# Two batches of near values and a tile's constant rows moved to GpSimd, across the border between two stages of a two-layer language-model kernel

## The reference, cut to what matters

```python
windows = [max(4, BLOCK_SIZE // 2 ** h) for h in range(H)]      # 256, 128, 64, 32, 16, 8, 4, 4, ...
qk = x @ Wqk + bqk
q, k = split(qk);  v = k                                        # the values are the keys
att = softmax(where(j <= i and j > i - window[h], q @ k.T / 4, -inf))
out = att @ v
gates = softmax(x @ Wgate + bgate)                              # one gate for each head
return (out * gates) @ Wproj + bproj
```

## Time and profile before

| | |
|---|---|
| median of the runs | 1427.9 us |
| profiled execution: its time, its span | 1427.86 us, 1426.1 us |
| PE, DVE, ACT, POOL busy | 1232.4, 849.3, 650.3, 666.0 us |
| mean granted TensorE clock | 0.925 of full |
| project_local, last PE instruction to last DVE instruction | 635.4 to 662.3 us |
| attend, first DMA to last DVE instruction | 662.8 to 801.9 us |

### The profile page before, as it was taken

The page is one execution under the profiler, slowest core; times in us unless marked ns, Lnnn a source line. Parts: engine busy times, 40 slices in busy tenths (PEclk is TensorE's granted clock), DMA queues, the critical chain, the costliest instruction groups (busy, mean ns, idle before and its releaser), DMA issues. The chain is left out here.

```text
span 1426.1 us, 29279 instructions
## 1 busy us (share of the span) xinstructions
PE 1232.4 (86%) x9695; PEld 967.0 (68%) x9696; DVE 849.3 (60%) x1794; ACT 650.3 (46%) x1253; POOL 666.0 (47%) x616
## 2 busy tenths in 40 slices
PE   6886999999978959972899796999689999989996
PEld 3664555555546747761667584999668888878885
DVE  5997788888827948996555494744323333333332
ACT  3881666666655635430354463333123333333332
POOL 7855777777361213787100000455225545444553
PEclk9995899999999977775999998999889999999998
DMA  2588999999400006563444320011275343545331
GB/s 56 172 255 264 253 273 276 278 282 270 111 2 1 1 28 184 173 202 94 91 113 95 110 83 30 23 30 37 68 268 133 55 110 80 139 129 137 51 53 19
DMA packets 122867, 179.27 MB, mean 126 GB/s; under 512 B 26052, under 2 KB 83820, under 8 KB 122772
## 3 DMA queue, kind: packets, MB, share of 16 engines
q1 hardware_dynamic: 105876, 159.62, 38.4%
q0 software_dynamic: 16896, 18.44, 7.9%
HBM read 104.73 MB, written 74.31 MB: 126 GB/s over the span
## 5 line engine op out<-in xcount | busy, mean ns | idle before, releaser
L1635 DVE TENSOR_REDUCE att_top<-att_psS 128x4 f32<-128x512 f32 (+2 forms) x192 | 195.2, 1037 | 46.8 <-PE att_psS L1522 43.7
L2791 POOL DMA_INDIRECT out<-ffn1c_y,ffn1c_table x72 | 113.3, 1574 | 180.8 <-ACT ffn1c_y L2904 92.1
L2932 DVE TENSOR_TENSOR ffn1c_hid<-ffn1c_psG,ffn1c_sil 128x512 f32<-128x512 f32 x72 | 49.8, 692 | 146.5 <-PE ffn1c_psG L2832 146.5
L1606 ACT ACTIVATE att_prob<-att_psS 128x1024 f32<-128x1024 f32 (+1 forms) x96 | 83.3, 888 | 64.9 <-PE att_psS L1536 64.9
L1516 PE MATMUL att_psS<-pairs_ka,pairs_qa 48*128 48x384 f32 (+3 forms) x512 | 100.3, 400 | 12.3 <-DMA pairs_ka<-k_parts 7.8
L2832 PE MATMUL ffn1c_psG<-ffn1c_w_h,ffn1c_xh 128*128 x288 | 97.9, 422 | 11.6 <-DMA ffn1c_w_l<-experts_lo 5.7
L1606 ACT ACTIVATE pairs_part<-att_psS 128x1024 f32<-128x1024 f32 (+1 forms) x96 | 82.8, 888 | 35.5 <-PE att_psS L1536 35.5
L2435 POOL DMA_INDIRECT slots<-ffn1b_entry,ffn1b_sloti x64 | 63.3, 989 | 65.7 <-ACT ffn1b_act_h L2648 54.1
L2780 POOL DMA_INDIRECT ffn1c_rows<-normed_rows,ffn1c_table x72 | 71.1, 987 | 45.4 <-DVE ffn1c_gate L2952 21.3
L2832 PE MATMUL ffn1c_psG<-ffn1c_w_l,ffn1c_xh 128*128 x288 | 91.5, 399 | 0.0
L2832 PE MATMUL ffn1c_psG<-ffn1c_w_h,ffn1c_xl 128*128 x288 | 91.3, 399 | 0.0
(11 more groups left out here) (397 smaller groups left out, 3505.4 us busy)
## 6 DMA issues: line engine op xcount, KB each, us to landing
prep_raw<-in_w_all SPq DMA_DIRECT2D x27, 512.0 KB, 5.4
experts_hi<-ffn0w_room SPq DMA_DIRECT2D x27, 512.0 KB, 5.6
experts_lo<-prep_lo SPq DMA_DIRECT2D x27, 512.0 KB, 6.6
ffn1c_w_h<-experts_hi SPq DMA_DIRECT2D x8, 1536.0 KB, 7.0
ffn1c_w_l<-experts_lo SPq DMA_DIRECT2D x8, 1536.0 KB, 11.4
qkv_near<-near_keys SPq DMA_DIRECT2D x32, 320.0 KB, 4.3
q_parts<-pairs_part SPq DMA_DIRECT2D x8, 1024.0 KB, 4.1
k_parts<-pairs_part SPq DMA_DIRECT2D x16, 512.0 KB, 5.9
```

Of the source, the lines that this page charges most:

```text
L1606: act.activation(dst, src, ACT.Exp, scale=0.25).then_inc(s["exp"], 1)
L1635: dve.tensor_reduce(dst, src, AX.X, ALU.max).then_inc(s["max"], 1)
L2791: pool.indirect_dma_start(out=rows_out, in_=y[:, t.buf, :], in_offset=None, out_offset=bass.IndirectOffsetOnAxis(ap=table[:, t.value:t.val ...
L2932: dve.tensor_tensor(hid[:, t.par, :], psG[:, t.par, 1, :], sil[:, t.par, :], ALU.mult).then_inc(s["act"], 1)
```

## The change

It has four parts.

1. `near`, `pv` and `pw` are allocated outside of both stages, so that they outlive `project_local`. POOL does the near values of batches 0 to 5 in `project_local`; those of batches 6 and 7 move to the start of POOL's list in `attend`. DVE's copy of the function, and its three instructions, are gone.
2. POOL's `third_term(7)` no longer waits for `near_products(7)`. For batches 0 to 6 that wait stays.
3. The four memsets of the constant rows go from DVE's list in `attend` to the front of POOL's.
4. PE waits for them at the first "B" of the block, and no longer ahead of its first "A".

Nothing of the shared expert is touched by the diff.

```diff
@@ project_local, POOL
             for b in range(B):
-                pool.wait_ge(s["prod"], b + 1)
+                if b < B - 1:
+                    pool.wait_ge(s["prod"], b + 1)
                 third_term(b)
-                if b >= 1:
+                if 1 <= b < B - 1:
                     near_values(b - 1)
-            pool.wait_ge(s["pv3"], B - 1)
+            pool.wait_ge(s["pv3"], B - 2)
+            pool.wait_ge(s["l"], B)
@@ project_local, DVE
-            def near_values(b):
-                dve.wait_ge(s["sdone"], 3 * b + 3)
-                dve.wait_ge(s["pv3"], b)
-                dve.tensor_tensor(pv[:]..., near[:, b % 3]..., pw[:, b % 2]..., ALU.mult).then_inc(s["pv1"], 1)
-                dve.wait_ge(s["pv1"], b + 1)
-                dve.tensor_tensor(pv[:, 0:2], pv[:, 0:2], pv[:, 2:4], ALU.add).then_inc(s["pv2"], 1)
-                dve.wait_ge(s["pv2"], b + 1)
-                dve.tensor_tensor(attn[:, tiles_of(b), PW:D], pv[:, 0], pv[:, 1], ALU.add).then_inc(s["pv3"], 1)
-                dve.wait_ge(s["pv3"], b + 1)
...
-            near_values(B - 1)
+            dve.wait_ge(s["sdone"], 3 * B)
@@ attend, POOL
+            def near_values(n, b):
+                if n:
+                    pool.wait_ge(s["near3"], n)
+                pool.tensor_tensor(pv[:]..., near[:, b % 3]..., pw[:, b % 2]..., ALU.mult).then_inc(s["near1"], 1)
+                pool.wait_ge(s["near1"], n + 1)
+                pool.tensor_tensor(pv[:, 0:2], pv[:, 0:2], pv[:, 2:4], ALU.add).then_inc(s["near2"], 1)
+                pool.wait_ge(s["near2"], n + 1)
+                pool.tensor_tensor(attn[:, TG * b:TG * (b + 1), PW:D], pv[:, 0], pv[:, 1], ALU.add).then_inc(s["near3"], 1)
+
+            for n in range(4):
+                pool.memset(ka[KROWS:KROWS + MROWS, n], -1.0).then_inc(s["const"], 1)
+            pool.wait_ge(s["const"], 4)
+            for n in range(2):
+                near_values(n, B - 2 + n)
             for b in range(B):
                 r = res[:, TG * b:TG * (b + 1), :]
                 pool.tensor_tensor(r, r, bias[:].unsqueeze(1).to_broadcast([P, TG, D]), ALU.add).then_inc(s["biased"], 1)
             pool.wait_ge(s["biased"], B)
+            pool.wait_ge(s["near3"], 2)
@@ attend, PE
-            pe.wait_ge(s["const"], 4)
...
                         if n == 0:
+                            if not v.after(1):
+                                pe.wait_ge(s["const"], 4)
                             pe.wait_ge(s["m_in"], 16 * v.value + 16)
@@ attend, DVE
-            for n in range(4):
-                dve.memset(ka[KROWS:KROWS + MROWS, n], -1.0).then_inc(s["const"], 1)
```

More of the change, by code:

```diff
@@ L578, in project_local @@
 def project_local(nc, res, ident, rstd, shift, w_qk, b_qk, w_g, b_g, q_dram, k_dram, v_dram, k_rows, gates, attn,
-                  b_out, bias_out):
+                  near, pv, pw, b_out, bias_out):
     with ExitStack() as ctx:
@@ L596, in project_local @@
         edge = k.sb("edge", [P, NW])
-        near = k.sb("near", [P, 3, NW, TG, DW])
         prod = k.sb("prod", [P, NW, TG, DW])
-        pv = k.sb("pv", [P, NW, TG, DW])
         smax, ssum = k.sb("smax", [P, TG, DH]), k.sb("ssum", [P, TG, DH])
-        pw = k.sb("pw", [P, 2, NW, TG, DH])
         psT = k.ps("psT", [P, KD, S])
@@ L1085, in make, with attend @@
         pool.wait_ge(s_done, n + 4 * len(self.windows))
-def attend(nc, tag, windows, bands, q_dram, k_dram, v_dram, m_dram, gates, ident, attn, res, bias):
+def attend(nc, tag, windows, bands, q_dram, k_dram, v_dram, m_dram, gates, near, pv, pw, ident, attn, res, bias):
     groups, HG = (len(windows), len(windows[0])) if windows else (NHG, H // NHG)
@@ L1119, in attend @@
         s_load, s_values = ([k.sem(f"{name}{n}") for n in range(2)] for name in ("load", "values"))
-        names = "const scoresA max topT_ps topT m_out m_in scoresB exp pv outT turned rec norm biased".split()
+        names = "const scoresA max topT_ps topT m_out m_in scoresB exp pv outT turned rec norm near1 near2 near3 biased".split()
         s = {n: k.sem(n) for n in names}
@@ L1128, in _ @@
         def _(pool):
+            def near_values(n, b):
+                if n:
+                    pool.wait_ge(s["near3"], n)
+                pool.tensor_tensor(pv[:].rearrange("p n t (h d) -> p (n t h) d", d=DK),
+                                   near[:, b % 3].rearrange("p n t (h d) -> p (n t h) d", d=DK),
+                                   pw[:, b % 2].rearrange("p n t h -> p (n t h)").unsqueeze(2).to_broadcast([P, NW * TG * DH, DK]),
+                                   ALU.mult).then_inc(s["near1"], 1)
+                pool.wait_ge(s["near1"], n + 1)
[7 more added lines that the diff above has]
+                near_values(n, B - 2 + n)
             for b in range(B):
@@ L3006, in tower @@
                     nc.sbuf_tensor("bias_out", [P, D], F32) as bias_out:
-                project_local(nc, res, ident, rstd1, shift1, a["w_qk1"], a["bqk"], a["w_g1"], a["bgate"], q1_dram, k1_dram, v1_dram, k_rows,
-                              gates, attn, a["bproj"], bias_out)
-                attend(nc, "att1", windows, bands, q1_dram, k1_dram, v1_dram, m_dram, gates, ident, attn, res, bias_out)
+                with nc.sbuf_tensor("near", [P, 3, NW, TG, DW], F32) as near, \
+                        nc.sbuf_tensor("near_values", [P, NW, TG, DW], F32) as pv, \
+                        nc.sbuf_tensor("near_shares", [P, 2, NW, TG, DH], F32) as pw:
+                    project_local(nc, res, ident, rstd1, shift1, a["w_qk1"], a["bqk"], a["w_g1"], a["bgate"], q1_dram, k1_dram, v1_dram,
+                                  k_rows, gates, attn, near, pv, pw, a["bproj"], bias_out)
+                    attend(nc, "att1", windows, bands, q1_dram, k1_dram, v1_dram, m_dram, gates, near, pv, pw, ident, attn,
+                           res, bias_out)
                 clear_semaphores(nc)
```

## The result

Ten runs of the changed kernel have a median of 1417.93 us (1414.55 to 1420.15), ten of the kernel before 1425.23 us. The ratio is 0.9939 with a 95% interval of 0.9925 to 0.9953: 8.7 us faster, 6.7 to 10.7. (The two medians by themselves stand 7.3 us apart, inside that interval.) The forecast was 1420.3 us and 7.6 us faster. The profiled execution took 1415.06 us, with a span of 1413.3 us, 12.8 less than before, so this pair of profiles shows more than the medians do.

The account below looks back on a forecast made before the run. PE, busy 86%, bounds most of the kernel; the hole at the project_local/attend border was the target. Terms 7.28 + 0 + 0.9 - 0.6 = 7.6 us, from 1427.9 to 1420.3 us, range 1417.5 to 1425.5.

Parts of the forecast that it names:

- The border term: Between project_local and attend: near values leave, SP's store wait arrives last, attend starts 7.28 us earlier.
- the constants: Start of attend: without DVE's memsets PE's first product waits for the last load instead, 0.9 us gained.
- the collision: In attend: the first two gate products wait under POOL's bias adds; half the second's wait charged, 0.6 us lost.
- the clock's pattern: PE's clock falls and rises early in attend; expected the same pattern, only moved, so 0 us.
- rival 3: Early attend: a clock fall or rise comes 3 us earlier or later, giving 1418.8 to 1423.3 us; chance 0.08.
- Part 2: End of project_local: DVE's near_products(7) goes first at the shared port, third_term(7) runs as before; worth 0 us.
- Rival 1: In attend: POOL keeps the port through all its bias adds, a gate product waits for all; 1428.5 us, chance 0.08.
- Rival 2: End of project_local: POOL goes first when batch 5's add ends, DVE gets its turn in attend; 1418.7 us, chance 0.14.
- rival 4: At the border: stores or the hop behind SP's wait take longer, the hole closes less; 1424.9 us, chance 0.12.

Follow-up runs that it names:

- part 4 alone: The kernel before, with only PE's wait for the constant rows moved to its first B, DVE keeping its memsets; ratio 0.9993 to the kernel before.
- part 1 alone: The kernel before, with only the near values of batches 6 and 7 moved to POOL's list in attend; ratio 0.996, 5.7 us faster.
- the changed kernel with sixteen adds: The changed kernel, with POOL's eight bias adds in attend cut into 16 short ones; ratio 0.9973 to the kernel before.
- the kernel with third_term early and sixteen adds: The changed kernel, with third_term(7) ahead of batch 5's two adds, those held until near_products(7) ends, and 16 short bias adds; ratio 0.9923 to the kernel before.

## Where the prediction failed, and where it was right

The border term held. What failed are the terms behind the border, and all three erred the same way. The sum had +0.9 us for the constants and -0.6 for the collision, and took the clock's pattern as unchanged. In the first pair of profiles the constants brought 1.6 us, the collision cost nothing, and the clock brought 1.3. From the end of the last near products to the end of attend the change took off 9.9 us (156.2 to 146.3), where the sum had 7.6; against the two later profiles of the changed kernel it is 9.7 and 9.1. The ratio's interval (6.7 to 10.7 us) can't tell 7.6 from 8.7, so the terms are judged by the profiles. The starting point failed too: 1427.9 us was the median of three runs, and ten runs gave 1425.2. That moved the forecast time up by 2.7 us and says nothing of the mechanism.

**Part 1, 7.28 us, right.** The mechanism was as told: SP's store wait became the last to arrive. From the end of the last near products to the first load it is 17.09 us in the three profiles without part 1, and 9.78 to 10.15, on average 9.97, in the eight with it and third_term(7) where it was. So it brought 7.1 us. The first load stood 13.5 us behind the start of the last near products, where I had said 12.9. I had read the hop behind the last engine as 0.50 us, from DVE. Behind SP it is 0.9, and 0.5 again where DVE is last.

**Part 2, 0, right, and for the reason given.** DVE was first at the port, POOL's instruction stood for its length, and putting the wait back changed nothing.

**Parts 3 and 4, 0.9 us, too small.** PE started 1.3 to 1.7 us earlier in all profiles with part 4. The step that failed took 3.3 us for the landing of the last load from the earlier trace rows; it took 2.5. The 3.3 us were not what the load takes beside DVE's memsets and POOL's bias adds: in part 4 alone the same load goes out beside both and lands in 2.2 us. They are scatter of the one profile that I had. The row of the DMA view of part 4 alone, at 667.56 us:

```profile
att_ka<-k_parts SPq DMA_DIRECT2D x1, 48.0 KB, 2.2
```

**The collision, 0.6 us, too large.** The step that failed charged half of the second gate product's wait. Behind the first gate product the kernel before and the changed one both have 105.36 us, with no wait in one and 2.13 and 0.59 us in the other, and waits up to 2.40 (first) and 2.00 us (second) cost nothing in any profile. Longer ones do: 3.90 us of wait cost 1.4 us, 4.61 cost 1.9, 5.73 cost 3.0, 6.11 cost 5.0, and 9.90 (of the first) cost 9.3. So DVE's idle time ahead of the next unit's scores gives back 2.5 to 2.7 us behind the second gate product in three of the four cases; why only 1.1 us in the fourth stays open.

**The clock, 0, off by 1.3 us in the first pair.** It is the small form of rival 3. All of the 1.3 us lie between PE's first product and the first gate product (27.16 against 25.86 us). That stretch has 27.2 and 27.8 us in the two profiles without part 4, 25.8 to 26.8 in eleven of the twelve with it, and 28.2 in the twelfth. So most of it may be scatter of this stage, and a part may belong to PE's earlier start; with two profiles on one side, and medians that show no gain for part 4, this stays open.

The terms by the profiles are 7.1 for the border and 1.5 for the constants, 8.6 us, and 0 for the collision; the clock comes on top, with a sign that changes from profile to profile. This fits the measured 6.7 to 10.7.

**Rival 1 was nearer than I thought.** I gave it 0.08 and called it all or nothing. The runs show both. With another add ready behind the one at work, DVE was let in at the next boundary 14 times, both gate products of the changed kernel's three profiles among them. It was passed over four times: the second gate product in three profiles, and the first in part 1 alone. Each of these four then waited until the whole row of adds was over. What decides was not found. It is not the gate product (the second was let in at the next boundary in five other profiles), and not how close to a boundary it asked: in the changed kernel with sixteen adds the first gate product asked 0.04 us behind the start of an add and was let in at its end, and in the kernel with third_term early and sixteen adds the second asked 0.46 us behind the start of one and was passed over. The case in part 1 alone is the closest one: it asked 0.02 us before the next add began.

**The rest.** Rival 2 did not occur in any profile. Of rival 4 the longer hop came true (0.9 us in place of 0.5), but the border as a whole closed as forecast, by the third column of the table. The rule of the Trainium skill (SBUF — State Buffer, "Who interferes with whom"), that the order of issue decides, held for the product of batch 7 against third_term(7). It does not fit the four gate products that were passed over: each had started, in the trace, before POOL's next add did, and the add went first. One reading of the prediction is off without effect: by the trace six of the eight near products start under an add, not five, since the one at 572.62 in the earlier trace rows starts 0.08 us before an add ends; the two that start under none take 2.82 us, and it takes 2.81.

## What to carry to other kernels

Look at what each engine waits for at a barrier between two stages: work of the slowest engine that nothing in the next stage reads early can move behind the barrier, and it gains the distance to the next latest engine, no more. Here that was SP's wait for its stores, and the gain 7.1 us. Before work is laid on POOL, list DVE's instructions with two inputs in SBUF in that stretch: they may wait for one POOL instruction or for the whole row of them, so what matters is how long the row is beside DVE's slack (2.5 to 2.7 us here), and cutting its instructions shorter did not help in the two kernels that did so. A semaphore wait that enforced an order which the shared port enforced anyway cost nothing here. And a load's time taken from one profile is one draw: here it read 3.3 us, and 2.2 to 2.7 in four others.

## What the runs showed of the hardware that was not expected

- A waiting DVE instruction with two inputs in SBUF is not always served when POOL's instruction ends. With eight adds of 2.31 us it was passed over once (4.61 us), with sixteen of 1.23 us twice, four times in a row each (5.73 and 6.11 us). In part 1 alone it asked at 686.80, 0.06 us ahead of a boundary between two adds, and waited for all of the next one (2.40 us), the last of the row. Once passed over, it was served only when the row was over.
- Two rows of 1536 bf16 elements take POOL 1.33 us to set, as long as DVE (1.34 us).
- One add of 128x8192 took 17.49 us, the same in eight pieces 18.53 and in sixteen 19.64: 0.14 to 0.15 us for each further instruction.
- The granted clock in attend's first 20 us differed between profiles of kernels that do the same there, and with it the time from PE's first product to the first gate product, 25.8 to 28.2 us.
